# Expert layer: slot table from one-hot products, gathers and scatters inside the expert stage, plain loads in the combining stage

## The reference

```python
def _L0_ffn_ref(x, gate_w, gate_b, w1, b1, w2, b2, gamma, beta):
    gate_logits = x @ gate_w + gate_b                     # 16 experts
    topk_vals, topk_idx = jax.lax.top_k(gate_logits, 2)
    topk_w = jax.nn.softmax(topk_vals, axis=-1)
    h = relu(einsum('bsh,ehf->bsef', x, w1) + b1)         # 256 -> 512
    expert_out = einsum('bsef,efh->bseh', h, w2) + b2     # 512 -> 256
    sel = take_along_axis(expert_out, topk_idx[..., None], axis=2)
    y = x + sum(topk_w[..., None] * sel, axis=2)
    return (y - mean(y)) / sqrt(var(y) + eps) * gamma + beta
...
x = x + _L0_ffn_ref(_layernorm(x)[None], ...)[0]
```

## Time and profile before

| | |
|---|---|
| median of 3 runs | 2957.73 us (2957.7 to 2966.04) |
| profiled execution, its own time | 2940.73 us |
| its span, first to last instruction | 2938.8 us |
| PE busy | 2559.6 us (87%) |
| DVE busy | 2112.4 us (72%) |
| ACT busy | 1795.7 us (61%) |
| POOL busy | 1501.9 us (51%) |

### The profile page before, as it was taken

One profiled execution on the slowest core, in us unless ns is written; L12 is line 12 of the kernel. 1 busy time (PEld: TensorE's weight loads), 2 busy tenths in 40 slices (PEclk: granted clock), 3 DMA queues, 4 the chain that ended last, 5 costly groups with the idle time before them and its releaser, 6 DMA issues. The chain is left out here.

```text
span 2938.8 us, 62138 instructions
## 1 busy us (share of the span) xinstructions
PE 2559.6 (87%) x20638; PEld 2082.3 (71%) x20725; DVE 2112.4 (72%) x4364; ACT 1795.7 (61%) x3207; POOL 1501.9 (51%) x1752
## 2 busy tenths in 40 slices
PE   6688888888972599638799999999959999999999
PEld 5466666666762599517677777777748888888888
DVE  5799999999963244265577877877766777777776
ACT  1688888888950133124366666666646777777775
POOL 5766666666623311382211121121147888888886
PEclk9799999999985799758899999999979999999999
DMA  5011111111134222211011111111000000000001
GB/s 199 20 39 46 49 38 38 38 38 38 38 116 157 74 71 70 72 47 51 6 41 56 38 38 57 38 38 57 20 6 0 0 0 0 0 0 0 0 0 38
DMA packets 53520, 122.55 MB, mean 42 GB/s; under 512 B 7402, under 2 KB 38734, under 8 KB 47822
## 3 DMA queue, kind: packets, MB, share of 16 engines
q1 hardware_dynamic: 46350, 102.28, 10.1%
q0 software_dynamic: 7104, 19.41, 2.0%
HBM read 97.39 MB, written 24.27 MB: 41 GB/s over the span
## 5 line engine op out<-in xcount | busy, mean ns | idle before, releaser
L1974 PE MATMUL f_pm<-f_wl,f_yt 128*128 128x256 f32 x2640 | 625.7, 380 | 0.0
L1974 PEld LDWEIGHTS f_pm<-f_wl,f_yt 128*128 128x128 f32 x2640 | 477.2, 191 | 51.6
L515 POOL TENSOR_SCALAR a_off<-ADJ 128x677 bf16<-128x677 f32 x88 | 300.0, 3431 | 254.4 <-DMA ADJ<-in_adj 242.7
L1022 POOL TENSOR_TENSOR ADJ<-ADJ,a_off 128x2708 f32<-128x2708 f32 x22 | 131.1, 5960 | 537.8 <-DVE ADJ L1101 537.8
L116 POOL TENSOR_SCALAR f_yy<-f_th,f_rs 128x255 f32<-128x255 f32 x660 | 366.9, 571 | 21.8 <-POOL f_rs L111 21.8
L1824 DVE SCALAR_TENSOR_TENSOR f_gg<-f_th,f_pm 128x512 f32<-128x512 f32 x319 | 218.8, 686 | 177.3 <-ACT f_th L1918 176.3
L588 DVE SCALAR_TENSOR_TENSOR a_lg<-a_fo,F,a_low 128x1024 f32<-128x1024 f32 (+1 forms) x264 | 297.6, 1155 | 46.4 <-ACT a_low L536 24.6
L1918 ACT ACTIVATE f_th<-f_pm 128x512 f32<-128x512 f32 x319 | 190.5, 597 | 200.5 <-PE f_pm L1974 200.5
L1081 DVE CUSTOM_DVE_ANT_0 a_sc<-a_qk,ADJ 128x1024 f32<-128x1024 f32 (+1 forms) x264 | 288.0, 1092 | 30.8 <-PE a_qk L1179 30.8
L679 PE MATMUL a_tp<-ident,a_lg 128*128 128x128 f32 x1936 | 265.5, 279 | 45.0 <-DVE a_wt L492 44.6
L1045 ACT ACTIVATE a_sc<-a_sc,a_mx 128x1024 f32<-128x1024 f32 (+1 forms) x264 | 277.8, 1052 | 42.4 <-DVE a_mx L1086 42.4
(11 more groups left out here) (256 smaller groups left out, 5013.2 us busy)
## 6 DMA issues: line engine op xcount, KB each, us to landing
ADJ<-in_adj SPq DMA_DIRECT2D x44, 1354.0 KB, 5.8
W<-in_L_ffn_w SPq DMA_DIRECT2D x32, 512.0 KB, 9.9
XD<-p_zeros SPq DMA_DIRECT2D x1, 7680.0 KB
m_rows<-XD SPq DMA_DIRECT2D x60, 128.0 KB, 2.0
YD<-m_y POOLq DMA_DIRECT2D x60, 128.0 KB, 2.0
out<-X SPq DMA_DIRECT2D x21, 128.0 KB
X<-in_x SPq DMA_DIRECT2D x3, 768.0 KB, 9.4
p_wqkv<-in_L_gnn_Wqkv SPq DMA_DIRECT2D x1, 768.0 KB, 4.5
```

Source lines behind the costliest of these rows:

```text
L515: pool.tensor_scalar(off[:, b, cols], adj[:, b, cols], 0.0, -HUGE, ALU.is_equal, ALU.mult).then_inc(off_done[b], 1)
L1974: mm = pe.matmul(out, yt[:, g, r, k, :], wl[:, k, :], start=(k == 0), stop=(k == KD - 1))
```

## The change

The slot table. In place of POSI (for each pick, its row in the sorted order) m0 now makes SLOT (for each row of the sorted order, which token stands there), two columns for each tile: the row of XD to read, and the row of YD to write. XD becomes the tokens in their own order with a row of zeros ahead (1 + 2708 rows), stored by SP in five plain transfers in m0. YD becomes the picks in token order, 1 + 2 x 2708 rows, with rows behind them for the empty places of the tiles. The duplicate rows of the last block are no longer routed, so `XTILES` falls from 60 to 58. The zero fill is gone.

```diff
-XTILES = (TOPK * NT * P + E * (P - 1)) // P + 1
+XTILES = (TOPK * N + E * (P - 1)) // P
...
-            sp.dma_start(keep["XD"].rearrange("(j p) d -> p j d", p=P),
-                         zeros[:, :].rearrange("p (a d) -> p a d", a=1).to_broadcast([P, XTILES, D])
-                         ).then_inc(xd_zero, 16)
```

```diff
+            for e in range(E):
+                mm = pe.matmul(pc[0:NA, e:e + 1], chosen[:, :, e], ones[:, 0:1], start=True, stop=True)
...
+                for j in range(NQ):
+                    mm = pe.matmul(pn[:, 0:2 * XTILES], in_row[:, q % 2, j, :],
+                                   named[:, q % 2, j, :, :].rearrange("p r x -> p (r x)"),
+                                   start=(q + j == 0), stop=(q == 3 and j == NQ - 1))
...
+                sp.dma_start(keep["XD"][1 + P * s0:1 + P * s1, :].rearrange("(t p) d -> p t d", p=P),
+                             XF[:, s0:s1, :]).then_inc(stored, 16)
...
-            for j in range(NA):
-                pool.indirect_dma_start(keep["XD"], bass.IndirectOffsetOnAxis(POSI[:, j:j + 1], 0),
-                                        XF[:, j % NT, :], None).then_inc(scattered, 16)
-            pool.wait_ge(scattered, 16 * NA)
+            pool.wait_ge(w_in, 48)
             pool.wait_ge(xf_done, NT)
+            with pool.Fori(0, NT) as t:
+                xs = X[:, bass.ds(t, 1), :]
+                pool.tensor_tensor(xs, xs, beta[:, :].rearrange("p (a d) -> p a d", a=1), ALU.add)
```

```diff
-                sp.dma_start(rows[:, b, :], keep["XD"][bass.ds((i * 2 + b) * P, P), :]).then_inc(rows_in[b], 16)
+            def gather(n):
+                i, b = divmod(n, 2)
                 if some(i):
+                    pool.wait_ge(turned[b], i)
+                pool.indirect_dma_start(rows[:, b, :], None, keep["XD"],
+                                        bass.IndirectOffsetOnAxis(SLOT[:, 0, n:n + 1], 0)).then_inc(rows_in[b], 16)
+
+            def scatter(n):
+                i, b = divmod(n, 2)
+                pool.wait_ge(y_done[b], i + 1)
+                pool.indirect_dma_start(keep["YD"], bass.IndirectOffsetOnAxis(SLOT[:, 1, n:n + 1], 0),
+                                        y[:, b, :], None).then_inc(stored[b], 16)
+            for n in range(4):
+                gather(n)
+            for n in range(XTILES):
+                if n + 4 < XTILES:
+                    gather(n + 4)
+                scatter(n)
...
-                dve.tensor_copy(y[:, b, :], p2[:, b, 0:D]).then_inc(y_done[b], 1)
+                dve.tensor_tensor(y[:, b:b + 1, :], p2[:, b:b + 1, 0:D], b2[:, bass.ds(e, 1), :],
+                                  ALU.add).then_inc(y_done[b], 1)
```

In m2 SP loads plain rows of YD (ten transfers, 768 KB for six blocks), PE has nothing left to do, and the work runs batch by batch, with four buffers for z and zz:

```diff
+            for b, (a, end) in enumerate(BATCHES):
+                s0, s1 = 2 * a, min(2 * end, NT - 1)
+                for k in range(TOPK):
+                    row = 1 + k * N
+                    sp.dma_start(got[:, k, s0:s1, :], keep["YD"][row + P * s0:row + P * s1, :].rearrange(
+                        "(t p) d -> p t d", p=P)).then_inc(loaded[b], 16)
...
             for k, (a, end) in enumerate(BATCHES):
-                dve.wait_ge(gathered[k], 16 * TOPK * 2 * (end - a))
+                dve.wait_ge(loaded[k], 16 * TOPK * (2 if 2 * end == NT else 1))
+                weigh(a, end)
+                dve.wait_ge(stats, 2 * end)
+                row_moments(dve, st, mom, 2 * a, 2 * end, folded, 3 * k).then_inc(moments, 1)
+                if k == 0:
+                    dve.wait_ge(w_in, 16)
+                else:
+                    scale(*BATCHES[k - 1])
+            scale(*BATCHES[-1])
```

More of the change, by code:

```diff
@@ L1278, in moe_route @@
         gb = ph.sb("gb", [P, E])
+        beta = ph.sb("beta", [P, D])
+        zero = ph.sb("zero", [1, D])
         ones = ph.sb("ones", [P, P])
         before = ph.sb("before", [P, P])
+        kept = ph.sb("kept", [P, 1])
         ie = ph.sb("ie", [P, E])
-        steps = ph.sb("steps", [P, NT])
-        tiles_i = ph.sb("tiles_i", [1, XTILES])
+        add_e = ph.sb("add_e", [P, NT])
+        steps = ph.sb("steps", [E, NT])
+        tiles_i = ph.sb("tiles_i", [E, XTILES])
+        rows_i = ph.sb("rows_i", [P, P])
+        starts_i = ph.sb("starts_i", [P, XTILES])
+        hi = ph.sb("hi", [P, TOPK, NT])
+        lo = ph.sb("lo", [P, TOPK, NT])
+        above = ph.sb("above", [NA, NA])
+        under = ph.sb("under", [E, 2, E])
         st = ph.sb("st", [P, NT, 6])
@@ new lines, in _ @@
+            dve.wait_ge(summed, 1)
+            dve.tensor_copy(total[:, :], pg[0:E, 0, 0:1]).then_inc(total_ok, 1)
+            dve.wait_ge(total_ok, 1)
+            link(dve.tensor_scalar(full[:, :], steps[:, :], total[:, :], None, ALU.is_lt))
+            dve.tensor_reduce(til[:, :], full[:, :], AX.X, ALU.add).then_inc(til_ok, 1)
+            dve.wait_ge(til_ok, 1)
+            dve.tensor_scalar(rise[:, :], under[:, 0, :], til[:, :], None, ALU.mult).then_inc(rise_ok, 1)
+            dve.wait_ge(based, 1)
@@ L1431, in _ @@
+            link(dve.tensor_copy(base[:, :], pg[:, 1, 0:E]))
             dve.wait_ge(ranks, 1)
@@ L1595, in y_out @@
             def y_out(i, b):
+                e = expert_of(dve, i, b)
                 dve.wait_ge(y_mm[b], i + 1)
@@ L1688, in _ @@
-        @block.tensor
-        def _(pe):
-            pe.wait_ge(w_in, 48)
-            for t in range(NT):
-                i, b = divmod(t, 2)
-                if some(i):
-                    pe.wait_ge(gt_sb[b], i)
-                pe.transpose(pt[0:E, b, 0:P], GD[:, t, :], ident[:, :]).then_inc(gt_ps[b], 1)
-                pe.wait_ge(gt_sb[b], i + 1)
-                if some(i):
-                    pe.wait_ge(third[b], i)
-                pe.matmul(pb[:, b, 0:D], gt[:, b, :], b2[:, :], start=True, stop=True).then_inc(b_mm[b], 1)
+                pool.wait_ge(moments, k + 1)
@@ L1702, in _ @@
+                inverse_deviation(pool, mom, rs, neg_half, 2 * a, 2 * end, pchain, 3 * k).then_inc(inv, 1)
+                if k:
+                    for t in range(2 * BATCHES[k - 1][0], 2 * BATCHES[k - 1][1]):
+                        residual(t)
+            for t in range(2 * BATCHES[-1][0], NT):
+                residual(t)
         @block.scalar
         def _(act):
-            for t in range(NT):
-                i, b = divmod(t, 2)
-                act.wait_ge(gt_ps[b], i + 1)
-                if some(i):
-                    act.wait_ge(b_mm[b], i)
-                act.copy(gt[:, b, :], pt[0:E, b, 0:P]).then_inc(gt_sb[b], 1)
@@ L1738, in _, with weigh @@
-            for k, (a, end) in enumerate(BATCHES):
-                dve.wait_ge(gathered[k], 16 * TOPK * 2 * (end - a))
-                with dve.Fori(a, end) as i:
-                    weigh(i)
-            dve.wait_ge(stats, NT)
-            row_moments(dve, st, mom, 0, NT, folded, 0).then_inc(moments, 1)
-            dve.wait_ge(w_in, 48)
-            for t in range(NT):
-                i, b = divmod(t, 2)
-                dve.wait_ge(z_done[b], i + 1)
-                if some(i):
-                    dve.wait_ge(x_out[b], i)
-                dve.tensor_tensor(zz[:, b, :], z[:, b, :], affine[:, 0, :], ALU.mult).then_inc(zz_done[b], 1)
+            def weigh(a, end):
+                for t in range(2 * a, 2 * end):
+                    dve.scalar_tensor_tensor(XF[:, t, :], got[:, 0, t, :], GW[:, 0, t:t + 1], XF[:, t, :],
+                                             ALU.mult, ALU.add).then_inc(first, 1)
+                    if t > 2 * a:
+                        second_part(t - 1)
+                    if t > 2 * a + 1:
+                        stat(t - 2)
+                second_part(2 * end - 1)
+                stat(2 * end - 2)
+                stat(2 * end - 1)
@@ new lines, in second_part, with stat, scale @@
+            def second_part(t):
+                dve.wait_ge(first, t + 1)
+                dve.scalar_tensor_tensor(XF[:, t, :], got[:, 1, t, :], GW[:, 1, t:t + 1], XF[:, t, :],
+                                         ALU.mult, ALU.add).then_inc(second, 1)
+            def stat(t):
+                dve.wait_ge(second, t + 1)
+                dve.bn_stats(st[:, t, :], XF[:, t, :]).then_inc(stats, 1)
+            def scale(a, end):
+                for t in range(2 * a, 2 * end):
+                    dve.wait_ge(z_done[t % 4], t // 4 + 1)
+                    if t >= 4:
+                        dve.wait_ge(x_out[t % 4], t // 4)
+                    dve.tensor_tensor(zz[:, t % 4, :], z[:, t % 4, :], gamma[:, :],
+                                      ALU.mult).then_inc(zz_done[t % 4], 1)
```

372 lines of the change are left out of this document (204 added, 168 removed).

## The result

| | before | after |
|---|---|---|
| median, us | 2958.89 (2957.7 to 2966.04, 4 runs) | 2837.01 (2834.12 to 2838.24, 4 runs) |
| profiled execution, us | 2940.73 | 2834.12 |
| span, us | 2938.8 | 2832.3 |

The ratio is 0.9582, 95% interval 0.9564 to 0.9599: 121.9 us less. Forecast were 2868 us and 2850 to 2890, so the kernel is faster than the range allowed. The two traces differ by 106.5 us and not by 121.9; that gap is the first thing that the experiments take up (1 and 2), and by them the change is worth 104.8 us.

What follows compares the result with a forecast made beforehand. Stages cannot overlap, each with its own bound: transfers and drains in m0 and m2, PE in m1. -48.4 + 1.2 - 42.6 = -89.8 took the profiled 2940.7 to 2850.9; plus 17.0 made 2868 us, range 2850 to 2890.

Steps and rivals of the forecast that it cites:

- the term of 17.0 us: Whole kernel: timed median stood 17.0 us above the profiled execution before, and this was added to the forecast sum.
- DRAIN's price: Stage ends: POOL's DRAIN costs 83 ns for each transfer POOL issued in the stage; 9.6 us forecast in m1.
- m1's end: Last part of m1: 0.6 us for a scatter replacing a store, 4.65 for DRAIN of 56 more transfers; together +5.2.
- m1's start: Start of m1: POOL's first gather starts later and shares the engines with the b2 load; +3.5 us, bounds +1 to +6.
- Two tiles: m1: 58 tiles instead of 60 at 3.73 us each, -7.5 us.
- m0: -48.4: m0: scatters and their drain give way to a table made by products; -48.4 us, bounds -52 to -42.
- DVE slowed beside POOL: POOL's additions of beta slow DVE's picks in m0, 1.0 us; in m2 DVE slowed beside POOL, 2.5 us.
- m2: -42.6: m2: no gathers, DVE sets the time; stage 61.9 us, so -42.6, with bounds of 54 to 74 us for the stage.
- Last moments: m2: DVE's last moments come 50.6 us after the stage's start, with loads there at 8 and 1.2 a block.
- the second rival: m2 gives less: DVE and POOL take each other's turns, loads come slowly; m2 74 us, time 2880; chance 0.12.
- the first (POOL as bound): m1: DVE's copies hold both POOL transfers of a tile, making POOL the bound; +12 to +19 us, 2880 to 2887; chance 0.15.
- The third (more is saved): Drain does not grow, b2 does not disturb, m2 at 55 us: -14 us, time 2854; chance 0.15.

Runs made afterwards that it cites:

- 1: The kernel before, unchanged, in 12 more timed runs: median 2940.44 us, profiled 2939.74 us.
- 2: The changed kernel, unchanged, run again beside the kernel before at 2940.82 us: 2836.00 us, ratio 0.9634.
- 3: The changed kernel with the 7680 KB zero fill put back, into a DRAM tensor that nothing reads: 2836.02 us.
- 5: The changed kernel with the load of the biases b2 held until the first two tiles' rows have landed: 2837.59 us.
- 11: The changed kernel with 60 tiles in m1 and not 58: 2843.57 us.
- 12: The changed kernel without POOL's 22 additions of beta in m0: 2834.15 us, m0 78.3 us.
- 9: The changed kernel with m2's 22 additions to X on DVE and not POOL: 2828.17 us, m2 50.5 us.
- 8: The changed kernel with m2's moments, inverse deviation and scaling done once over 22 blocks, not in four batches: 2835.23 us, m2 58.8 us.
- 10: The changed kernel with a third POOL transfer in every m1 tile, a scatter nothing reads: 2856.35 us, m1 253.0 us.
- 4: The changed kernel with 30, 104, 112 and 130 unread scatters ending POOL's work in p0, m0, m2, p1; 130 gave DRAIN 1.45 us; no kernel time given.

## Why the prediction missed

The kind of gain and its places were right: m0 and m2 lose their transfers, m1 stays PE's, turns 3.73 us apart. The total missed by 31 us. The step that failed first is the term of 17.0 us: with the same width of range around 2850.9 the measured 2837 would have lain inside. The second is DRAIN's price. All steps (together they make some 34 us; the median of after stands 2.9 above its trace, which is the rest):

- **"I carry that over": 17.0 us, wrong.** Nothing that repeats lies between timed and profiled runs. I had three timed runs and one profiled one that disagreed, and built a term on the difference. What made those first runs of before 17 to 25 us longer stays open; three of 12 later ones were 8 us longer than the rest, and the runs of after spread by 5 us at most. The fill is excluded (1, 3). Nor was everything slow: the four runs of after from that time, 2834.1 to 2838.2, are where its later runs are. The four chips that followed agree; the first runs' chip is not known.
- **m1's end: "56 x 83 ns = 4.65", with 0.6 for the scatter +5.2; measured -4.1.** Last turn to end of stage: 12.35 us for 16.46. The three drains of the earlier trace rows agreed at 83 ns, and that price held in every stage of up to 112 transfers; the stage has 116. I had extrapolated a line from 44 and 60 to 116, past a point where it starts again: DRAIN took 0.63 us and not 9.6. This is 9.3 us, more than the errors of m0, m2 and m1's start together (2.7, 3.4 and 1.0).
- **m1's start: +3.5; measured +4.5** at the third turn (up to +6.3 in the other traces with this m1), about within the bounds of +1 to +6. The place was right (the gather beside b2), and a cure by order alone showed how the two transfers hurt each other (5). Two tiles: -7.5, right (11).
- **m0: -48.4; measured -51.1.** One-column products 4.5 us, measured 2.6, under the lower bound of 2.8; the products behind them 5.5, measured 6.2; DVE slowed beside POOL 1.0, measured 0.07 (12). One-hots 15.5, measured 15.4; last products to SLOT 3.0, measured 2.8; end of stage 1.0, measured 0.9.
- **m2: -42.6; measured -46.0.** Last moments at 50.6, measured 47.5: loads there at 7.3 and not 8, a block 1.1 us and not 1.2. Tail and end 11.3, measured 11.0. The estimate was about right, but it had too little for what POOL's additions do: 2.5 us for DVE slowed beside them, where taking them off POOL saved 8.1 (9). POOL's additions were not merely last: they doubled each of DVE's products that ran beside them, 10 of 22 here and nearly all in (8). That is the double price of the second rival, on a part of the instructions.
- The stages before m0 -1.05, where 0 to -1 was said for p0, and those behind -1.2: both within what traces of one code differ by.
- Smaller slips: the last PE products of m0 ended 36.4 us after the picks began, where 41 was written; the sum's own steps have SLOT ready at 41. And the bounds of m0, the start and m2, simply added, span 2854 to 2889 and not 2856 to 2882.

Of the rivals, the first (POOL as bound) would have needed a third transfer a tile (10); the holding up by copies on which it rested is real, but small. The third (more is saved) pointed to the right side, but it had DRAIN not grow; it shrank.

What the change gave by part was not run alone: that m0 lost 51 us by the scatters and their DRAIN, and m2 46 by the gathers, is read from the two traces; only that the batches of m2 gave nothing (8), that the additions of beta cost m0 nothing (12) and what two tiles cost (11) was tested.

## What to carry to other kernels

Before a constant offset between timed and profiled runs goes into a forecast, it has to repeat. A price per item read from small counts (a drain, a ring) is safe only inside the counts seen: look for where it resets. And when two engines show the same raised mean on the same shape, try giving one of them both jobs: m2 fell from 58.6 to 50.5 us by moving work onto its busiest engine.

## What the runs showed that I had not expected

- DRAIN after POOL's transfers: 82 ns for each since the stage's start or, from the 114th on, since that one; 104 transfers cost 8.6 us at the stage's end, 116 cost 0.6. In front of the 114th POOL stood still 3.0 us longer than usual in one stage of back-to-back scatters (4), and not at all in another (10).
- Beside a load of 2048 KB in rows of 16 KB a gather of 128 KB is there only 6.4 to 8.5 us after its issue (2.7 to 3.0 for the first two in (5), where the load waits). With the load in 16 pieces in rows of 1 KB the gathers took 4.2 and 4.5 us, the first turn came 3.3 us sooner, and the load itself took 11.2 us for 8.4. Whether the size of the rows did it, or that SP issues the pieces over 7.7 us, was not told apart.
- An indirect transfer of POOL that overlaps DVE's copy of 128x1024 float32 takes up to 0.5 us longer, 0.1 in the mean (10).
- Starting PE sooner after a long idle time gave back under half: it ran its first 32 products at 1.2 GHz. With filler of 1.11 us behind the last table products and 2.93 us ahead of the first tile the granted clock was 0.50 from 936 to 938, under the second filler, and 1.00 from 940 on, when the 32 products came.
- A power on POOL grows with its columns, 1.2 us for four and 3.89 for 22.
